# A new table of slots for the order of work in the attention phase

## The reference

```python
h = layernorm(x)
q, k = rope(h @ Wq + bq), rope(h @ Wk + bk);  v = h @ Wv + bv
probs = softmax(where(causal, q @ k.T / sqrt(16), -inf))
x = x + layernorm((probs @ v) @ Wo + bo)
h = layernorm(x)
gate = sigmoid(h @ gate_w + gate_b);  top 2 of 16, divided by their sum
y = h + mlp(h, shared) + sum(gate_e * mlp(h, expert e) for the two)
x = x + layernorm(y)
```

## Time and profile before

| what | us |
|---|---|
| median of 3 runs (lowest, highest) | 2628.42 (2620.87, 2629.79) |
| the profiled execution | 2620.87 |
| its span, first to last instruction | 2619.1 |
| mean granted TensorE clock | 0.966 |
| busy TensorE, VectorE, ScalarE, GpSimd | 2389.8, 1981.9, 1510.6, 1637.4 |
| turn 5 (340.44 to 394.47) | 54.03 |
| turn 18, the longest (1049.96 to 1112.81) | 62.85 |

### The profile page before, as it was taken

One profiled execution on the slowest core, in us unless ns is written; L12 is line 12 of the kernel. 1 busy time (PEld: TensorE's weight loads), 2 busy tenths in 40 slices (PEclk: granted clock), 3 DMA queues, 4 the chain that ended last, 5 costly groups with the idle time before them and its releaser, 6 DMA issues. The chain is left out here.

```text
span 2619.1 us, 60730 instructions
## 1 busy us (share of the span) xinstructions
PE 2389.8 (91%) x18798; PEld 1576.4 (60%) x18798; DVE 1981.9 (76%) x5220; ACT 1510.6 (58%) x3420; POOL 1637.4 (63%) x2761
## 2 busy tenths in 40 slices
PE   4999999999999999899999999997279999999997
PEld 2565566655666555555655665554168777877664
DVE  5678888888888888777888888874347777776887
ACT  1566676666766666566666766665124444444655
POOL 2446666666656666666666656643266666666887
PEclk7899999999999999999999999999579999999999
DMA  4354435544455443444434444332346556554997
GB/s 125 91 149 134 134 119 158 163 129 129 131 150 162 127 128 111 135 144 146 144 117 122 132 144 148 107 108 76 71 146 181 149 152 198 157 154 154 305 352 243
DMA packets 288653, 388.00 MB, mean 148 GB/s; under 512 B 27923, under 2 KB 238099, under 8 KB 288213
## 3 DMA queue, kind: packets, MB, share of 16 engines
q1 hardware_dynamic: 260788, 308.56, 39.8%
q0 software_dynamic: 27552, 75.57, 8.4%
HBM read 193.40 MB, written 172.27 MB: 140 GB/s over the span
## 5 line engine op out<-in xcount | busy, mean ns | idle before, releaser
L847 ACT ACTIVATE probs<-ps_a 128x512 f32<-128x512 f32 (+1 forms) x1408 | 736.8, 561 | 354.1 <-PE ps_a L731 288.0
L967 DVE TENSOR_REDUCE negmax<-ps_d 128x2 f32<-128x768 f32 (+3 forms) x768 | 782.3, 1040 | 199.5 <-PE ps_d L715 184.8
L713 PE MATMUL ps_d<-ks,qs 96*128 96x128 bf16 (+3 forms) x2048 | 483.9, 305 | 75.9 <-DVE negmax L967 50.5
L729 PE MATMUL ps_a<-qs,ks 99*128 99x512 bf16 (+3 forms) x2048 | 525.4, 304 | 1.4 <-ACT probs L847 0.3
L731 PE MATMUL ps_a<-mask_exp,ident_bf 128*128 128x128 bf16 x2048 | 396.3, 221 | 0.0
L715 PE MATMUL ps_d<-mask_max,ident_bf 128*128 128x128 bf16 x2048 | 394.4, 222 | 0.0
L1367 POOL DMA_INDIRECT y_dram<-ysb,to_row x286 | 282.4, 987 | 118.3 <-issue 76.8
L713 PEld LDWEIGHTS ps_d<-ks,qs 96*128 96x128 bf16 x2048 | 203.0, 99 | 232.8 <-DVE negmax L967 76.6
L743 PE MATMUL ps_out<-probs,va 128*32 128x512 f32 (+3 forms) x4096 | 329.5, 440 | 0.0
L1440 PE MATMUL ps_gu<-wgu,rows_t 128*128 x1144 | 303.7, 389 | 11.5 <-issue 9.0
L729 PEld LDWEIGHTS ps_a<-qs,ks 99*128 99x128 bf16 x2048 | 201.5, 98 | 168.1 <-issue 59.9
(11 more groups left out here) (200 smaller groups left out, 4520.9 us busy)
## 6 DMA issues: line engine op xcount, KB each, us to landing
qs<-q_stack_dram SPq DMA_DIRECT2D x128, 384.0 KB, 5.0
rows<-sorted_dram SPq DMA_DIRECT2D x286, 129.0 KB
y_in<-y_dram SPq DMA_DIRECT2D x32, 1024.0 KB
q_stack_dram<-q_parts SPq DMA_DIRECT2D x64, 384.0 KB
x_in<-in_x SPq DMA_DIRECT2D x32, 512.0 KB
q_stack_dram<-q_parts SPq DMA_DIRECT2D x64, 256.0 KB
x<-in_x SPq DMA_DIRECT2D x32, 512.0 KB
h_dram<-h SPq DMA_DIRECT2D x32, 512.0 KB, 3.0
```

Of the source, the lines that this page charges most:

```text
L713: pe.matmul(ps_d[:, number % 2, at:at + width], qs[0:KR, b % 2, h, j * P:(j + 1) * P], ks[0:KR, b % 2, g, 0:width], start=True, stop=False)
L729: pe.matmul(ps_a[:, number % 3, at:at + width], ks[0:KM, b % 2, g, j * P:(j + 1) * P], qs[0:KM, b % 2, g * HG + h0 + k, j * P:T], start=Tr ...
L847: act.activation(probs[:, at:at + nh * width], ps_a[:, number % 3, 0:nh * width], ACT.Exp) \
L967: dve.tensor_reduce(negmax[:, g // 2, j, at:at + nh], src, AX_X, ALU.max, negate=True) \
```

## The change

MISC, MAX_AT, SUMS_AT and SIDE get new slots. No step is added or removed, and no other line changes.

```diff
@@ -63,70 +63,70 @@
 
 
 MISC = {
-    (0, 2): [("xt", 0, 2)],
-    (0, 5): [("xt", 1, 2)],
-    (0, 6): [("ot", 0, -1)],
-    (0, 7): [("ot", 1, -1)],
+    (0, 3): [("xt", 0, 2)],
+    (0, 6): [("xt", 1, 2)],
+    (0, 7): [("ot", 0, -1), ("ot", 1, -1)],
     (0, 9): [("cn", 0, -2), ("at", 0, -1), ("at", 1, -1)],
     (0, 10): [("op", 0, -1)],
     (1, 1): [("op", 1, -1)],
-    (1, 7): [("qe", 0, 2), ("qe", 1, 2), ("mt", 1, 0)],
-    (2, 9): [("kk", 0, 2)],
-    (3, 2): [("ht", 0, -1), ("ht", 1, -1)],
-    (3, 4): [("rg", 0, -1)],
-    (3, 7): [("mt", 0, 1), ("vt", 0, 2)],
-    (3, 8): [("rt", 0, -1)],
+    (1, 7): [("qe", 0, 2), ("qe", 1, 2)],
+    (1, 8): [("mt", 1, 0)],
+    (2, 8): [("kk", 0, 2)],
+    (3, 5): [("ht", 0, -1), ("ht", 1, -1)],
+    (3, 7): [("rg", 0, -1), ("mt", 0, 1)],
+    (3, 9): [("rt", 0, -1)],
+    (3, 10): [("vt", 0, 2)],
 }
 
-MAX_AT = [[0, 0, 1, 3, 8, 10], [0, 1, 3, 6, 8, 9], [0, 1, 4, 6, 7, 9], [1, 1, 3, 7, 8, 8]]
-SUMS_AT = [10, 4]
+MAX_AT = [[0, 1, 3, 5, 9, 10], [0, 1, 4, 5, 8, 9], [0, 1, 2, 5, 8, 9], [0, 0, 4, 5, 7, 9]]
+SUMS_AT = [10, 5]
 
 SIDE = {
-    "load_stacks": (0, 5),
-    "load_x_res": (0, 6),
-    "load_x": (0, 5),
-    "store_q0": (2, 4),
-    "store_h2": (3, 10),
-    "store_q1": (3, 10),
-    "store_k": (3, 10),
+    "load_stacks": (0, 6),
+    "load_x_res": (1, 5),
+    "load_x": (1, 6),
+    "store_q0": (1, 10),
+    "store_h2": (3, 9),
+    "store_q1": (2, 1),
+    "store_k": (3, 9),
     "scatter0": (0, 9),
-    "scatter1": (0, 10),
-    "scatter2": (1, 1),
-    "scatter3": (1, 3),
-    "root_proj": (1, 2),
-    "root_2": (2, 6),
-    "root_1": (3, 10),
-    "split0a": (1, 2),
-    "split0b": (1, 9),
-    "split0c": (2, 2),
-    "split1a": (2, 7),
-    "split1b": (3, 2),
-    "split1c": (3, 7),
+    "scatter1": (1, 0),
+    "scatter2": (1, 2),
+    "scatter3": (1, 4),
+    "root_proj": (1, 3),
+    "root_2": (1, 10),
+    "root_1": (3, 8),
+    "split0a": (1, 3),
+    "split0b": (1, 5),
+    "split0c": (1, 7),
+    "split1a": (2, 3),
+    "split1b": (2, 5),
+    "split1c": (3, 1),
     "split2a": (3, 9),
-    "split2b": (3, 10),
-    "split2c": (3, 10),
+    "split2b": (3, 9),
+    "split2c": (3, 9),
     "norm_proj_a": (1, 9),
     "norm_proj_b": (1, 9),
     "norm_2_a": (2, 10),
-    "norm_2_b": (2, 10),
-    "norm_1_a": (3, 8),
-    "norm_1_b": (3, 10),
-    "weigh_choice_a": (0, 2),
-    "weigh_choice_b": (0, 5),
+    "norm_2_b": (3, 2),
+    "norm_1_a": (3, 9),
+    "norm_1_b": (3, 9),
+    "weigh_choice_a": (0, 3),
+    "weigh_choice_b": (0, 6),
     "plan_ends": (0, 9),
     "plan_tiles": (1, 0),
-    "plan_limits": (1, 3),
-    "stats_proj_a": (1, 2),
+    "plan_limits": (1, 1),
+    "stats_proj_a": (1, 1),
     "stats_proj_b": (1, 4),
-    "moments_proj": (1, 5),
-    "add_residual_a": (1, 10),
-    "add_residual_b": (1, 10),
-    "stats_2_a": (1, 10),
-    "stats_2_b": (2, 0),
-    "moments_2": (2, 4),
-    "stats_1_a": (3, 4),
-    "stats_1_b": (3, 4),
-    "moments_1": (3, 6),
+    "moments_proj": (1, 6),
+    "add_residual_a": (1, 9),
+    "add_residual_b": (1, 9),
+    "stats_2_a": (1, 9),
+    "stats_2_b": (2, 1),
+    "moments_2": (2, 1),
+    "stats_1_a": (2, 7),
+    "stats_1_b": (3, 0),
+    "moments_1": (3, 0),
     "choose": (3, 10),
 }
```

## The result

The changed kernel takes 2647.90 us (median of 4 runs, 2644.68 to 2649.00), the kernel before 2629.11 in the same comparison: ratio 1.0068, interval 1.0052 to 1.0085. It is slower, as forecast, and by half as much: 18.8 us where I had said 2666, 37 above that median. The profiled execution took 2651.59, its span 2649.8.

The account below looks back on a forecast made before the run. TensorE sets the turn, so reordering changes only its waits and clock: about +1.0 us a turn, 28, plus 3 for end turns and 14 for the clock, on 2620.87, gives 2666 us; range 2608 to 2696, the forecast's own 2645 to 2685.

Parts of the forecast that it names:

- The order: All reordering effects on TensorE's waits: about +1.0 us a turn, 28 us for 28 turns.
- Group 2: VectorE's wait before M(1,2): four short waits become one of 2.36 us, +0.1 a turn.
- the load behind mt: Load of the mt rows, issued 0.9 later; any lateness for E(2,0) hidden by the 2.36 wait, costed at nothing.
- Group 3: ScalarE's clump of norm_2_b, heads_t and ht copies: 0.81 us of waits, net +0.58 a turn.
- The turn's start: All four norm_1 activations ahead of E(3,10), so E(0,1) waits for its buffer: +0.24 us (0 to 0.6).
- The ot pair: The two ot steps stand together and the counts wait for VectorE's work on the second: +0.3 us (0 to 0.5).
- the small waits: Groups 0 and 1, M and P steps spread more evenly: some 0.2 us of short waits goes (0 to 0.4).
- the turns at either end: Turns outside the 28 turns 2 to 29: 3 us added to the sum.
- The clock: TensorE's clock falls after the 2.36 pause in half of 28 turns, 1.3 us each, less old falls: +14 us.
- Rival 1: The clock holds, as after the pause of 1.94: 2648 us, chance 0.22.
- the expert phase: Everything after 1850 us: not touched, costed at nothing.
- Rival 3: Faster: the transfer burst thins and late completions on ScalarE and before the second qe go, -28 us, 2593; chance 0.18.

Follow-up runs that it names:

- undo_group2: Changed kernel with group 2 back in its old order of M and kk, P steps left at slot 5: 2585.89 us against 2563.45 for the kernel before, ratio 1.0094.
- split_residual_3: Kernel before with VectorE's residual and statistics block taken apart and norm_2_a ahead of kk's copy on ScalarE: 2519.84 us against 2560.03, ratio 0.9831.
- undo_scalar: Changed kernel with norm_2_b, both ht transposes and norm_1 back in their old slots: 2587.84 us against 2563.45 for the kernel before, ratio 1.0099.
- misc_back: Changed kernel with MISC, norm_2_b, norm_1 and weigh_choice as before, only kk staying at (2,8): 2668.36 us against 2625.44 for the kernel before, ratio 1.0159.
- after_again: Changed kernel run again without edit: 2648.18 us against 2625.20 for the kernel before, ratio 1.0087.
- before_again: Kernel before run again without edit: 2561.82 us against 2563.45, ratio 0.9998.
- only_group2: Kernel before with only group 2's order of M and kk's slot changed as in the change: 2647.39 us against 2625.20, ratio 1.0075.
- mid_pause: Changed kernel with M(1,1) and M(1,2) moved into slot (2,0): 2712.98 us against 2625.20 for the kernel before, ratio 1.0322.

## Why the prediction was right on the order and wrong on the clock

What bounds the kernel was read rightly. TensorE's waits and its clock were the whole matter, and the places where the new order moves the waits were those of the forecast.

*The order*, forecast at +1.0 a turn, measured +0.86. Term by term:

- Group 2: four waits become one and nothing is won, forecast +0.1, measured -0.10. M(1,2) comes after one wait of 1.8 and another of 0.3 at E(2,0), for the load behind mt; I had put 2.36 in one piece and called this load hidden. Its effect was hidden, but it split the pause. undo_group2 shows that the sum does not hang on the order of M, split_residual_3 that it goes when VectorE's block is taken apart.
- Group 3: forecast 0.81 of waits (E(3,4) 0.27, E(3,7) 0.46, E(3,10) 0.08), measured 0.30, 0.34 and 0.21, 0.85. The stretch grew by 0.73, forecast 0.58. The size was right, the cause only in part: undo_scalar shows that 0.26 of it goes away with the slots of norm_2 and ht that I named, and misc_back that as much waiting stays without them, part of it behind M(2,0) and M(2,1) ahead of E(3,1).
- The turn's start, +0.24 for E(0,1): measured 0.08. In the change E(0,1) starts 0.83 after E(0,0), in undo_scalar, with norm_1 in two halves and the same matmuls between, 0.75.
- The ot pair, +0.3: a wait of 0.23 before the counts, some 0.1 of it new, and group 0 longer by 0.20, with the 0.08 at E(0,1) and the small waits I had counted off included.

With 3 us for the turns at either end (1.4 and 2.4 measured) the order was put at 31 us and came to 28.6 in the profile, the 0.1 of the clock included.

*The clock* is the step that failed: "With one pause of 2.36 in every turn I take a fall in half of the 28 turns", 14 falls at 1.3, +14 us. There were 3, at 1.5 each, for 4 at 1.1 before: 0.1 us. Two things are wrong in it. The pause itself is 1.64 of idle (1.8 start to start), where I had 2.36 in one piece. And I read a chance out of the length of three single pauses (2.68, 2.08, 1.94), all in padding turns or at the end of the phase, where length alone does not give it: 4 falls in 23 turns at 2.10, 19 at 2.15, and 3 to 9 at 1.64. How the miss divides between the two is not shown. Rival 1, where the clock holds, is nearest to what happened. That its 2648 is the measured median to the digit is luck: it counts the 4 old falls as gone, where 3 came in their place, and starts 8 us below the median of before.

*The base.* I added the sum to the profiled execution, 2620.87, and left the median, 8 us higher, aside. Between the two profiled executions the forecast was +45 us and the measured difference 30.7; the clock's 14 are nearly all of the gap. Without them 2620.87 + 31 = 2652 stands beside 2651.59, which is closer than the sum deserves: the order came out 2.4 lower, and the expert phase, costed at nothing, 2.0 higher. The rest of the way from 2666 to 2647.90 is that the profiled execution of the change lay 4 us above its median, as that of before lay 8 below. (All 29 executions of the change in that comparison have a median of 2646.0, from 2640.83 to 2655.60.) So the medians differ by 18.8 only, and by 23.0 in after_again. Most of what executions of one kernel differ by goes with their mean clock (before_again).

*Rival 3* rested on thinning the burst of transfers. The late copy still waits 60.6 us in 28 turns, for 70.5; the second qe's stretch did not shrink (+0.04). The lateness does not follow from the order alone, since at the faster speed it is absent with the same instructions.

## What to carry to other kernels

Where a list fixes the order of all engines, a wait on a slower engine's block is not moved away by reordering the waiters: find the block and take that apart, then look at each engine's own queue for what now stands behind something unrelated, as norm_2 stood behind kk's copy. A pause that is gathered from several short ones can cost the clock even with the same sum (7 falls in only_group2, 3 in the change, 4 before); work out its length first, and do not read the odds from the length alone. A forecast for a median starts from a median, or says how the execution it starts from stands to it.

## What the runs showed of the hardware

- The same program took 2.4% less in some comparisons than in others (2563 and 2625 us); whether this is the chip is not shown. Of a steady turn it was 0.55 us, with TensorE's work seen about 2 us late behind scatters in the slower ones and not in the faster; turns 19 to 21 with padding took 54.6 in place of 58.3, and the expert phase 737 in place of 770.
- After single pauses of TensorE of 1.64 us the granted clock fell to 0.51 in 3 to 9 turns of 23, after 2.10 in 4, after 2.15 in 19, after 2.83 in all. A fall of 3.4 us cost 1.1 us a turn in the kernel before, where waits follow it, and 1.5 in the change, where none do; one of 6.8 us cost 2.2 to 2.3 in mid_pause.
